# The order of the layer phase's steps is replaced by another list

## What is computed

```
def _layer(x, ...):
    h = shift_token(x)                     # second half of the columns comes from the token before
    q, k, v = split(h @ wqkv)              # 8 heads of 64
    q = l2norm(q) * qs; k = l2norm(k) * ksc
    q, k = rotary_xpos(q, k)
    x = x + local_attention(q, k, v) @ wo  # window 128: own block of 128 keys and the one before
    h = layernorm(shift_token(x)) * lg + lb
    a, g = split(h @ w1 + b1)
    return x + (a * gelu(g)) @ w2 + b2
out = x + attention(xn) + layer1(layer0(xn))
```

## Time and profile before

| | |
|---|---|
| median of 3 runs | 2031.27 us (2028.2 to 2031.36) |
| the profiled execution's own time | 2028.86 us |
| its span | 2027.0 us |
| PE busy / DVE / ACT / POOL, of the span | 92% / 63% / 68% / 46% |
| mean granted clock of PE | 0.982 |

### The profile page before, as it was taken

One profiled execution on the slowest core, in us unless ns is written; L12 is line 12 of the kernel. 1 busy time (PEld: TensorE's weight loads), 2 busy tenths in 40 slices (PEclk: granted clock), 3 DMA queues, 4 the chain that ended last, 5 costly groups with the idle time before them and its releaser, 6 DMA issues.

```text
span 2027.0 us, 47841 instructions
## 1 busy us (share of the span) xinstructions
PE 1861.7 (92%) x17808; PEld 1566.4 (77%) x17808; DVE 1283.9 (63%) x4125; ACT 1382.6 (68%) x3997; POOL 926.9 (46%) x1315
## 2 busy tenths in 40 slices
PE   6999999999999779999999999999999999989998
PEld 5777777777777568778787787887877878778787
DVE  5544543444444467777677777777777777777775
ACT  5886877778677465765756757667576575675764
POOL 2532542434334563635626536355365562553632
PEclk9999999999999889999999999999999999999999
DMA  3321231312224410110110101304101112111110
GB/s 128 110 80 63 79 112 51 98 59 91 80 80 154 163 45 27 38 51 22 46 53 19 46 17 48 118 14 163 53 20 61 32 46 64 26 49 30 36 45 27
DMA packets 127003, 128.91 MB, mean 64 GB/s; under 512 B 28112, under 2 KB 101940, under 8 KB 126772
## 3 DMA queue, kind: packets, MB, share of 16 engines
q1 hardware_dynamic: 123604, 119.56, 18.9%
q10 hardware_dynamic: 3168, 6.29, 0.9%
HBM read 72.84 MB, written 37.25 MB: 54 GB/s over the span
## 4 chain that ended last, share of the span: by engine, by line
DVE 21%; PE 21%; ACT 19%; POOL 3%; issue 2%; DVEq 0%; POOLq 0%; ACTq 0%; SPq 0%
PE f_bank L1409 8%; ACT f_prob L1645 8%; DVE f_u L1799 5%; PE f_scores L1561 3%; DVE f_gu L1795 3%; PE f_bank L1546 3%; ACT f_u L1665 3%; DVE f_norm L1689 2%; POOL f_prob L1362 2%; DVE f_scores L1733 2%; ACT f_probT L1584 2%; PE f_scores L1488 2%; ACT f_square L1616 2%; DVE f_qk_tok L1711 2%; DVE f_qk_tok L1708 1%
## 5 line engine op out<-in xcount | busy, mean ns | idle before, releaser
L589 POOL TENSOR_SCALAR a_prob<-a_prob,a_row_inv,a_gate 128x128 f32<-128x128 f32 x512 | 224.4, 455 | 408.1 <-DVE a_row_inv L929 408.1
L1362 POOL TENSOR_SCALAR f_prob<-f_prob,f_row_inv 128x192 f32<-128x192 f32 x512 | 232.2, 472 | 334.5 <-DVE f_row_inv L1741 334.5
L1409 PE MATMUL f_bank<-weights,f_actT 128*128 128x512 f32 x1152 | 306.7, 408 | 21.0 <-DVE f_norm L1689 11.1
L1546 PE MATMUL f_bank<-f_hT,f_w 128*128 128x256 f32 x2112 | 275.4, 285 | 12.5 <-DVE f_gu L1795 12.5
L1546 PEld LDWEIGHTS f_bank<-f_hT,f_w 128*128 128x128 f32 x2112 | 261.2, 190 | 20.0 <-DVE f_gu L1795 18.7
L1409 PEld LDWEIGHTS f_bank<-weights,f_actT 128*128 128x128 f32 x1152 | 208.5, 192 | 78.4 <-DVE f_norm L1689 16.7
L1645 ACT ACTIVATE f_prob<-f_scores,f_neg_max 128x192 f32<-128x192 f32 x512 | 207.7, 423 | 21.3 <-DVE f_neg_max L1733 19.6
L1338 POOL TENSOR_TENSOR f_norm<-f_norm,f_minus_half 128x16 f32<-128x16 f32 x64 | 192.9, 3014 | 37.8 <-DVE f_norm L1693 36.2
L1665 ACT ACTIVATE f_u<-f_gu 128x256 fp32r<-128x256 f32 x192 | 80.2, 418 | 183.8 <-DVE f_gu L1795 183.8
L821 ACT ACTIVATE a_prob<-a_scores,a_neg_max 128x128 f32<-128x128 f32 x512 | 179.5, 390 | 27.8 <-DVE a_neg_max L920 26.5
L612 PE MATMUL a_bank<-a_xT,weights 128*128 128x512 f32 x768 | 194.1, 405 | 1.5 <-DVE a_wgate L898 1.5
(11 more groups left out here) (139 smaller groups left out, 4074.3 us busy)
## 6 DMA issues: line engine op xcount, KB each, us to landing
split_weights<-a_hi_lo SPq DMA_DIRECT2D x16, 512.0 KB, 2.8
x_next<-states SPq DMA_DIRECT2D x32, 256.0 KB, 3.2
tables<-scaled_tables SPq DMA_DIRECT2D x16, 512.0 KB, 5.5
f_x<-states SPq DMA_DIRECT2D x16, 512.0 KB, 4.7
split_weights<-a_hi_lo SPq DMA_DIRECT2D x12, 682.0 KB, 4.0
weights<-split_weights ACTq DMA_DIRECT2D x6, 1024.0 KB, 8.4
f_w<-split_weights SPq DMA_DIRECT2D x4, 1280.0 KB, 11.1
f_v_crossed<-f_v SPq DMA_DIRECT2D x40, 128.0 KB, 2.3
```

The costliest lines, as they stand in the source:

```text
L589: last = nc.gpsimd.tensor_scalar(part, part, row_inv[:, a % 2, head, t:t + 1], gate[:, half, t, h:h + 1], ALU.mult, ALU.mult)
L1362: last = nc.gpsimd.tensor_scalar(part, part, row_inv[:, a % 2, head, t:t + 1], 1.0, ALU.mult, ALU.mult)
L1409: last = nc.tensor.matmul(out, lhs(c, a), rhs(c, b), start=(i == 0), stop=(i == len(order) - 1))
L1546: mm = nc.tensor.matmul(out[:, which * PART:(which + 1) * PART], w1[:, wp, c, col:col + P], hT[:, hp, c, columns_of(a // FH)], start=(i == ...
```

## The change

Only the list `ORDER` is replaced. Both lists hold the same steps, so every instruction, buffer and kind of wait stays; the values waited for follow from the positions. The attention phase and the opening steps of the layer phase (`before`) keep their order. The full diff:

```diff
-ORDER = [("scores", 0), ("scores", 1), ("softmax", 0), ("softmax", 1), ("weigh", 0), ("weigh", 1), ("transpose_x", 0), ("load_x", 0),
-         ("scores", 2), ("transpose", 0), ("softmax", 2), ("scores", 3), ("weigh", 2), ("weigh", 3), ("load_x1", 0), ("transpose", 1),
-         ("softmax", 3), ("load_tables", 0), ("load_others", 0), ("project_qk", 0), ("rope", 0), ("scores", 4), ("values", 0), ("values", 1),
-         ("take_o", 0), ("transpose", 2), ("project_qk", 1), ("softmax", 4), ("scores", 5), ("weigh", 4), ("transpose", 3), ("rope_sum", 0),
-         ("project_qk", 2), ("values", 2), ("softmax", 5), ("scores", 6), ("weigh", 5), ("values", 3), ("rope", 1), ("take_o", 1),
-         ("transpose", 4), ("scores", 7), ("softmax", 6), ("transpose_qk", 0), ("weigh", 6), ("project_qk", 3), ("shift_keys", 0),
-         ("project_o", 0), ("rope_sum", 1), ("weigh", 7), ("transpose", 5), ("values", 4), ("values", 5), ("softmax", 7), ("take_o", 2),
-         ("rope", 2), ("shift_front", 0), ("transpose", 6), ("project_v", 0), ("ln_stats", 0), ("transpose_qk", 1), ("transpose", 7),
-         ("ln_apply", 0), ("values", 6), ("values", 7), ("take_o", 3), ("project_v", 2), ("transpose_h", 0), ("project_o", 1), ("rope_sum", 2),
-         ("up", 0), ("shift_back", 0), ("up", 1), ("up", 2), ("ln_stats", 1), ("project_v", 1), ("ln_apply", 1), ("down", 0), ("project_v", 3),
-         ("up", 3), ("rope", 3), ("x1_bias", 0), ("down", 1), ("down", 2), ("transpose_h", 1), ("cross_values", 0), ("load_wqkv", 0), ("up", 4),
-         ("up", 5), ("down", 3), ("add_attended", 0), ("up", 6), ("up", 7), ("up", 8), ("up", 9), ("rope_sum", 3), ("down", 4),
-         ("transpose_qk", 2), ("down", 5), ("up", 10), ("down", 6), ("up", 11), ("down", 7), ("down", 8), ("transpose_qk", 3), ("out", 0),
-         ("down", 9), ("down", 10), ("down", 11), ("out", 1)]
+ORDER = [("scores", 0), ("transpose_x", 0), ("softmax", 0), ("scores", 1), ("weigh", 0), ("softmax", 1), ("weigh", 1), ("scores", 2),
+         ("transpose", 0), ("scores", 3), ("weigh", 2), ("softmax", 2), ("project_qk", 0), ("transpose", 1), ("values", 0), ("softmax", 3),
+         ("load_tables", 0), ("rope", 0), ("weigh", 3), ("scores", 4), ("project_qk", 1), ("transpose", 2), ("values", 1), ("rope_sum", 0),
+         ("take_o", 0), ("scores", 5), ("softmax", 4), ("load_x1", 0), ("transpose", 3), ("weigh", 4), ("project_qk", 2), ("scores", 6),
+         ("rope", 1), ("values", 2), ("load_others", 0), ("values", 3), ("softmax", 5), ("take_o", 1), ("weigh", 5), ("transpose", 4),
+         ("load_x", 0), ("scores", 7), ("softmax", 6), ("project_qk", 3), ("weigh", 6), ("project_o", 0), ("transpose", 5), ("rope_sum", 1),
+         ("shift_front", 0), ("values", 4), ("weigh", 7), ("softmax", 7), ("values", 5), ("take_o", 2), ("shift_keys", 0), ("transpose_qk", 0),
+         ("transpose_qk", 1), ("transpose", 6), ("ln_stats", 0), ("transpose", 7), ("values", 6), ("values", 7), ("rope", 2), ("ln_apply", 0),
+         ("take_o", 3), ("project_v", 2), ("transpose_h", 0), ("project_o", 1), ("rope_sum", 2), ("up", 0), ("up", 1), ("up", 2),
+         ("project_v", 1), ("down", 0), ("shift_back", 0), ("project_v", 0), ("ln_stats", 1), ("ln_apply", 1), ("project_v", 3),
+         ("cross_values", 0), ("down", 1), ("rope", 3), ("up", 3), ("down", 2), ("transpose_h", 1), ("up", 4), ("up", 5), ("down", 3), ("up", 6),
+         ("rope_sum", 3), ("transpose_qk", 2), ("down", 4), ("x1_bias", 0), ("up", 7), ("down", 5), ("down", 6), ("up", 8), ("up", 9),
+         ("up", 10), ("up", 11), ("add_attended", 0), ("down", 7), ("down", 8), ("transpose_qk", 3), ("down", 9), ("down", 10), ("load_wqkv", 0),
+         ("out", 0), ("down", 11), ("out", 1)]
```

## The result

| | before | after |
|---|---|---|
| median | 2030.7 us | 2111.5 us |
| ratio of the times, with its 95% interval | | 1.0387 (1.0369 to 1.0406) |
| the profiled execution's own time / span | 2028.9 / 2027.0 | 2103.6 / 2101.8 |
| mean granted clock of PE | 0.982 | 0.962 |

A forecast was written before the change was run, and what follows sets the result against it. PE was taken to bound the kernel (busy 92% of the span). 15 halves at +2.0 us give 30, plus 1 for the clock, on 2028.9: 2060 us, with an 8-in-10 range of 2014 to 2088.

The forecast's parts named there:

- both places: PE's new waits before the third scores (2.5 to 3 us idle) and in `transpose` 3 (1 us or more on POOL).
- the signs that were to show it: Listed trace signs: load behind x copies, waits at third scores, `transpose` 3 and `transpose_h` 0, L1689 waits nearly gone, 83-84 us halves.
- the middle part: Up to `transpose` 5: spread fills remove projection and softmax waits, against new waits at `transpose` 1 to 3; -2.0 us a half.
- Start of a half: ACT's table load falls behind the x copies, delaying Exp and the third scores; +1.4 us a half at equal work.
- The walk: Stepping the new list through one half, engines in list order with old step lengths; +1.0 us a half without the meeting.
- The meeting: After `rope` 0, POOL's `weigh` 3 and DVE's `rope_sum` 0 start together and disturb each other; +1.0 us, ends 0.4 and 2.4.
- rival 2: POOL and DVE take turns where they meet, +2.4 for +1.0, with late `weigh` steps: 51 us, 2080; chance 0.22.
- the end of 2.4: Upper end for `weigh` 3 beside `rope_sum` 0: taking turns, `weigh` 3 ends 2.4 us later and `transpose` 3 waits.
- The clock: PE's clock drops after a half's start in more halves; a few tenths per dip, 0 to 5 us in all, 1 taken.
- `transpose_h` 0: PE arrives before its layer norm input, held by POOL's `rope` 2 multiplies: 1.45 us waiting, +1.5 us a half.
- rival 1: Old waits were dearer: early load saves 1.3 a half, `rope` 2 not holding `ln_apply` 1.4; 2019, down to 2000; chance 0.25.
- The FFN part: From `transpose_h` 0 to the next scores: `project_v` 0 behind `down` 0, `up` 7 waits +0.25; -0.7 us a half.

The follow-up runs named there:

- e4: New list plus idle PE transposes, 18 before the third scores of a half and 9 before each head of `transpose` 3; ratio 1.0217, median 2074.4 us.
- e15: New list plus 18 idle PE transposes before the third scores of a half only; ratio 1.0303, median 2087.3 us.
- e7: Old kernel plus 6 idle PE transposes before the third scores of each half; ratio 0.9986 to the old kernel.
- e13: New list with `transpose_x` 0 behind `weigh` 1, `rope_sum` 0 behind `weigh` 4, `ln_apply` 0 ahead of `rope` 2; ratio 0.9913, median 2008.6 us.
- e12: e8 with `rope` 0 moved behind `project_qk` 1 and `rope_sum` 0 behind `weigh` 4; ratio 1.0234, median 2073.4 us.
- e8: New list with `transpose_x` 0 behind `weigh` 1, `weigh` 3 ahead of `rope` 0, `ln_apply` 0 ahead of `rope` 2; ratio 0.9949, median 2017.6 us.
- e9: e8 plus 6 idle PE transposes before the third scores of each half; ratio 0.9900, median 2007.1 us.

## Why the prediction was right and where it was wrong

**The side and both places were right.** Of the signs that were to show it these are there: the load behind the copies, 2.95 us before the third scores (2.5 to 3 forecast), more than 1 us of POOL in `transpose` 3. Halves of 83 to 84 us are not, they are 84 to 90. The waits of the projections for L1689 (11.1 us in all) are gone, as the middle part had it.

**Start of a half: right.** The walk had Exp at 3.9 and the third scores at 5.55; measured 3.91 and 5.69. At the first projection it is late, 10.3 for 9.0, and 1.1 of those 1.3 us are scores and transposes at the lower clock, not waiting.

**The meeting: the value taken was too small.** The step said "I take +1.0 ... and keep 0.4 and 2.4 as ends". Measured is +1.94, near the end at which the two take turns, which stood as rival 2. The row chosen, 1092.78 in the earlier trace rows, showed one POOL instruction behind two DVE instructions in a row, not a chain of turns. By the rule of the Trainium skill (SBUF — State Buffer, "Who interferes with whom"), cited there, the end of 2.4 would have been the term; the trace agrees with it more than with the row that I preferred, since each add held one POOL instruction for a turn. The argument against turns was misread as well. The row of 1.44 starts at 1096.56, when POOL's first multiply (1095.35, 1.25 long) was ending, so it was held by the second alone. In the new trace two instructions of `ln_apply` stand behind the same two multiplies and take 1.37 each, one turn per multiply.

**The clock: the term that failed.** The step said "one dip costs a few tenths, 0 to 5 us in all, 1 taken". Measured: 35 us come back when PE is merely kept busy in the two gaps (e4), 17 of them in the first (e15). The page's busy time of PE, 32 us more for the same matmuls, says the same. No row stood behind the few tenths; the one row of a fall, shows PE at half speed for some 3.5 us, and e7 later got only 3 us back for 8 of lost clock in the old list. In the new list a fall comes at a wait of 3 us, in front of work that PE alone sets, and there are 24 falls for 8; the walk itself had gaps of 2.9 and 1.3 us in each half. Filled, the list has 17 falls fewer and takes 35 us less, about 2 us for each. That more halves would have one was said; that each would cost more than tenths, and that the gap in `transpose` 3 would bring its own, was not.

With 35 for 1 and the meeting at 1.94 for 1.0 (14 us over 15 halves) the sum would have been 2028.9 + 30 + 14 + 35 = 2108, against 2109 by the ratio. The split fits too: 30 + 14 = 44 of waiting, and PE is idle for 43 us more. That it fits to 1 us is partly luck, since the next term was some 10 us too large and something not found makes up for it.

**`transpose_h` 0: the wait was smaller, the step matters more.** Forecast 1.45 of waiting; measured 0.54 in this half, where PE itself came at 51.3 and not at 46.05, and 0.9 in the mean (13.4 us over 15 halves, 1.4 before). The cosine multiplies do hold `ln_apply`, as said: its second and third instructions take 1.37 for 0.34, and undoing it brings 16 us, for the 21 that rival 1 gave to it (1.4 x 15).

**The FFN part: right.** The walk had 35.1 us from `transpose_h` 0 to the next scores (82.6 less 47.5); measured 1159.94 less 1124.95 = 34.99. It was 34.23 before, without the 1.5 us of `project_v` 0.

## What to carry to other kernels

A gap of the bounding engine is not priced by its length: here a gap of about 3 us cost nearly as much again in slow matmuls behind it (17 of the 36 us of the first stall), and idle transposes in the gap bought that back. When two queues are reordered, look for the moment at which one event releases both DVE and POOL on SBUF operands, and keep such pairs apart; see that a table load can run while its engine waits anyway. And a single time for a whole new order hides this: the places of three of its 110 steps cost 96 us, while the list with these three moved is 0.9% under the old one (e13).

## What the runs showed of the hardware

- Four POOL instructions of 0.40 us and two adds of DVE of 1.23, released together, take turns instruction by instruction: 3.56 for 1.62 us on POOL (3.55 in e12), about 0.2 more on DVE. Two instructions of `ln_apply` and two multiplies of POOL do the same (1.37 for 0.34, twice). The Trainium skill (SBUF — State Buffer, "Who interferes with whom") has the blocking by whole instructions; what sets the turns no run here shows.
- The clock went to 1.2 GHz in the last microsecond of a wait of 2.95 us or up to 1.5 us behind it, and also where two waits of 1.55 and 1.26 us had two transposes between them. In e8 it fell at 6 of the starts, behind a wait of 0.94 us; 6 transposes there cut the wait to 0.28, no start had a fall, and the lost clock went from 24 to 3 us (e9).
- A fall does not cost its lost clock everywhere: 55 less 12 us of it were worth 35 us (e4), 24 less 3 were worth 10 (e9), 15 less 7 worth 3 (e7).
